# A transformer megakernel on one core: three rotating buffers for queries and keys, their low parts written in place, two for the rounded keys

## The reference, cut to what matters

```python
def _attn(q, k, v, mask):
    scale = 1.0 / np.sqrt(HD)
    s = jnp.einsum('bqhd,bkhd->bhqk', q, k) * scale
    s = jnp.where(mask, s, jnp.finfo(s.dtype).min)
    a = jax.nn.softmax(s, axis=-1)
    return jnp.einsum('bhqk,bkhd->bqhd', a, v)
```

## Time and profile before

| | |
|---|---|
| runs of the kernel | 1174.65, 1185.07, 1185.32 us (median 1185.07) |
| the profiled execution | 1176.95 us, its span 1174.8 us |
| PE busy | 1074.7 us (91% of the span), weight loads 725.9 us |
| DVE, ACT, POOL busy | 744.3, 622.1, 618.1 us |
| granted clock of PE | 0.856 of full on average |
| transfers on SP's queue | 24.3% of 16 engines' span |

### The profile page before, as it was taken

One profiled execution on the slowest core, in us unless ns is written; L12 is line 12 of the kernel. 1 busy time (PEld: TensorE's weight loads), 2 busy tenths in 40 slices (PEclk: granted clock), 3 DMA queues, 4 the chain that ended last, 5 costly groups with the idle time before them and its releaser, 6 DMA issues.

```text
span 1174.8 us, 32004 instructions
## 1 busy us (share of the span) xinstructions
PE 1074.7 (91%) x12961; PEld 725.9 (62%) x12961; DVE 744.3 (63%) x1852; ACT 622.1 (53%) x938; POOL 618.1 (53%) x739
## 2 busy tenths in 40 slices
PE   7898899989998999999999999889888988897998
PEld 5455555656666676676666566656555655565676
DVE  7757856767666443777778566767777754565521
ACT  2134434565656655454455455655556765654653
POOL 6657757665565432112226567665577553465531
PEclk9669968988777999999999667887889987876899
DMA  6423322332232102000000323232332323222101
GB/s 233 146 70 111 126 83 83 125 124 90 84 118 82 46 28 90 10 7 6 11 12 30 103 70 111 84 98 95 118 123 96 118 89 114 83 80 72 59 28 45
DMA packets 101459, 96.89 MB, mean 82 GB/s; under 512 B 11632, under 2 KB 93808, under 8 KB 100928
## 3 DMA queue, kind: packets, MB, share of 16 engines
q1 hardware_dynamic: 101312, 94.84, 24.3%
HBM read 18.77 MB, written 2.15 MB: 18 GB/s over the span
## 4 chain that ended last, share of the span: by engine, by line
PE 60%; POOL 12%; SPq 9%; issue 8%; DVE 6%; DMA 2%; ACT 2%; POOLq 0%; ACTq 0%; DVEq 0%
PE weighed L725 11%; PE scores L896 6%; PE row_scores L658 5%; PE weighed L748 5%; SPq L2135 4%; SPq L2138 4%; PE scores L695 4%; PE scores L613 3%; PE scores L710 3%; DVE negmax L1217 3%; PE row_scores L896 3%; PE quads L620 2%; POOL kblk_r L1927 2%; DMA q_ring<-qr 2%; PE quads L605 2%
## 5 line engine op out<-in xcount | busy, mean ns | idle before, releaser
L1217 DVE TENSOR_REDUCE negmax<-row_scores 128x8 f32<-128x616 f32 (+1 forms) x312 | 299.9, 961 | 248.7 <-PE row_scores L658 203.2
L1733 ACT ACTIVATE p<-scores 128x1024 f32<-128x1024 f32 (+1 forms) x253 | 251.6, 1019 | 145.3 <-PE scores L710 141.0
L1927 POOL TENSOR_TENSOR kblk_r<-work,pack_const 128x308 fp32r<-128x308 f32 (+1 forms) x160 | 133.9, 838 | 197.3 <-PE row_scores L658 183.2
L725 PE MATMUL weighed<-p,v 77*32 77x128 f32 (+1 forms) x5120 | 213.9, 319 | 2.1 <-DVE nat L1233 1.3
L725 PEld LDWEIGHTS weighed<-p,v 77*32 77x32 f32 (+1 forms) x5120 | 157.4, 127 | 57.9 <-issue 45.1
L658 PE MATMUL row_scores<-kblk_r,qr 32*128 32x308 f32 (+1 forms) x624 | 161.0, 511 | 16.6 <-DVE negmax L1217 13.4
L695 PE MATMUL scores<-q_ring,k_ring 32*77 32x128 f32 (+1 forms) x2512 | 136.4, 284 | 39.4 <-ACT p L1733 31.2
L695 PEld LDWEIGHTS scores<-q_ring,k_ring 32*77 32x77 f32 (+1 forms) x2512 | 112.1, 194 | 48.0 <-ACT p L1733 35.9
L658 PEld LDWEIGHTS row_scores<-kblk_r,qr 32*128 32x128 f32 x624 | 68.5, 214 | 104.1 <-DVE negmax L1217 49.9
L710 PE MATMUL scores<-nblk,select 32*77 32x512 bf16 (+1 forms) x628 | 104.2, 463 | 0.0
L1970 POOL TENSOR_TENSOR attn<-nat,rden 128x128 f32<-128x128 f32 x160 | 65.0, 406 | 61.5 <-DVE rden L1238 61.1
(11 more groups left out here) (334 smaller groups left out, 2027.4 us busy)
## 6 DMA issues: line engine op xcount, KB each, us to landing
q_ring<-work SPq DMA_DIRECT2D x160, 128.0 KB, 2.1
q_ring<-qr SPq DMA_DIRECT2D x160, 128.0 KB, 2.1
k_ring<-k_high SPq DMA_DIRECT2D x64, 128.0 KB, 2.1
k_ring<-work SPq DMA_DIRECT2D x64, 128.0 KB, 2.1
k_ring<-k_high SPq DMA_DIRECT2D x96, 77.0 KB, 2.0
k_ring<-work SPq DMA_DIRECT2D x96, 77.0 KB, 2.0
shared<-gates_hbm SPq DMA_DIRECT2D x24, 256.0 KB, 3.2
shared<-in_ctx_tok SPq DMA_DIRECT2D x15, 154.0 KB
```

The source lines that it names most:

```text
L725: mm = e.matmul(av_bank[TILE * j:TILE * j + TILE, i2 * S:(i2 + 1) * S], v[0:nk, at:at + TILE], p[n % 2][0:nk, g * NJ + j, :], start=i1 == ...
L1217: e.tensor_reduce(negmax[q % 2][:, 2 * h:2 * h + 2, s * NJ:(s + 1) * NJ], row_banks(n, h)[:, :, 0:NJ * nk].rearrange("p g (j k) -> p g j k ...
L1733: e.activation(p[n % 2][0:nk, 8 * h:8 * h + 8, :], score_banks(n, h)[0:nk].rearrange("p g (j q) -> p (g j) q", j=NJ), ACT.Exp, bias=hide, ...
L1927: e.tensor_tensor(kblk_r[n % 2][:, 0:NJ * nk].rearrange("p (j k) -> p j k", j=NJ), k_of[q % 2][:, s * nk:(s + 1) * nk].unsqueeze(1).to_bro ...
```

## The change

Queries and keys get three buffers each, used in turn (`q_of[q % 3]`, `k_of[q % 3]`), in the nine slices of `work` that held two each and the two low parts. The low part is written over the value itself. The rounded keys get two buffers of their own. What waited for the landing of the quad before (`round_k`, `split_q`, `split_k`) now waits for the quad two before (`round_k`), or for nothing of that kind (the splits); the writers of a buffer wait for the landing of the quad three before, through the new helper `stacked`. `split_k` now overwrites what `spread_k` reads, so it waits for the fourth `spread_k` of its quad. For the first quad of each phase it moves one slot later for that.

```diff
-        xn, q_of, k_of = [work[:, j, :] for j in range(3)], [work[:, 3 + j, :] for j in range(2)], [work[:, 6 + j, :] for j in range(2)]
-        q_low, k_low = work[:, 5, :], work[:, 8, :]
-        k_high = sb("k_high", [128, QUAD * S], F32R)
+        xn, q_of, k_of = ([work[:, 3 * i + j, :] for j in range(3)] for i in range(3))
+        k_high = [sb(f"k_high{i}", [128, QUAD * S], F32R) for i in range(2)]
...
+        def stacked(w, q):
+
+            for m in (2 * q, 2 * q + 1):
+                if m >= 0:
+                    w.wait_ge(*pair_landed(m))
...
             def rotate(q, which):
...
-                w.wait_ge(*freed)
-                if which:
-                    w.wait_ge(kblk_r_done, 4 * (q - 2) + 4)
+                stacked(w, q - 3)
...
             def round_k(q):
...
-                w.wait_ge(k_split, q)
-                if q:
-                    w.wait_ge(*pair_landed(2 * q - 2))
-                    w.wait_ge(*pair_landed(2 * q - 1))
-                e.copy(k_high[:, 0:cols], k_of[q % 2][:, 0:cols]).then_inc(k_rounded, 1)
+                w.wait_ge(k_split, q - 1)
+                stacked(w, q - 2)
+                e.copy(k_high[q % 2][:, 0:cols], k_of[q % 3][:, 0:cols]).then_inc(k_rounded, 1)
...
             def split_q(q):
                 w.wait_ge(qr_done, q + 1)
-                if q:
-                    w.wait_ge(*pair_landed(2 * q - 2))
-                    w.wait_ge(*pair_landed(2 * q - 1))
-                e.tensor_tensor(q_low, q_of[q % 2], qr[q % 3][:, :].bitcast(F32), ALU.subtract).then_inc(q_split, 1)
+                e.tensor_tensor(q_of[q % 3], q_of[q % 3], qr[q % 3][:, :].bitcast(F32), ALU.subtract).then_inc(q_split, 1)
 
             def split_k(q):
                 cols = QUAD * layer_of(q).nk
                 w.wait_ge(k_rounded, q + 1)
-                if q:
-                    w.wait_ge(*pair_landed(2 * q - 2))
-                    w.wait_ge(*pair_landed(2 * q - 1))
-                e.tensor_tensor(k_low[:, 0:cols], k_of[q % 2][:, 0:cols], k_high[:, 0:cols].bitcast(F32),
+                w.wait_ge(kblk_r_done, 4 * q + 4)
+                e.tensor_tensor(k_of[q % 3][:, 0:cols], k_of[q % 3][:, 0:cols], k_high[q % 2][:, 0:cols].bitcast(F32),
                                 ALU.subtract).then_inc(k_split, 1)
...
                     if t == 4 * lo - 5:
                         split_q(lo)
-                        split_k(lo)
-                    if cl == 0 and qi + 1 in quads and qi + 1 != lo:
-                        split_q(qi + 1)
+                    if cl == 0 and qi + 1 in quads:
+                        if qi + 1 != lo:
+                            split_q(qi + 1)
                         split_k(qi + 1)
```

More of the change, by code:

```diff
@@ L1184, in rotate @@
                 live = 0 if which == 0 else 1
-                dst = (q_of, k_of)[which][q % 2]
-                proj, freed = ((proj_q, (q_split, q - 1)), (proj_k, (k_split, q - 1)))[which]
+                dst, proj = ((q_of, proj_q), (k_of, proj_k))[which]
+                dst = dst[q % 3]
                 bank = k_bank(q) if which else quad_bank[:, :]
@@ L1208, in take_q @@
                 w.wait_ge(proj_q, q + 1)
-                w.wait_ge(q_split, q - 1)
-                e.tensor_scalar(q_of[q % 2], quad_bank[:, :], W[layer.name + "_qb"], None, ALU.add).then_inc(q_done, 1)
+                stacked(w, q - 3)
+                e.tensor_scalar(q_of[q % 3], quad_bank[:, :], W[layer.name + "_qb"], None, ALU.add).then_inc(q_done, 1)
             def row_max(n, h):
@@ L1645, in round_q @@
                 w.wait_ge(rows_done, 8 * (q - 3) + 8)
-                if q >= 3:
-                    w.wait_ge(*pair_landed(2 * (q - 3) + 1))
-                e.copy(qr[q % 3][:, :], q_of[q % 2]).then_inc(qr_done, 1)
+                stacked(w, q - 3)
+                e.copy(qr[q % 3][:, :], q_of[q % 3]).then_inc(qr_done, 1)
             def round_k(q):
@@ L1677, in take_k @@
                 w.wait_ge(proj_k, q + 1)
-                w.wait_ge(k_split, q - 1)
-                w.wait_ge(kblk_r_done, 4 * (q - 2) + 4)
+                stacked(w, q - 3)
                 if layer.mask == "kv":
-                    done = e.copy(k_of[q % 2][:, 0:cols], quad_bank[:, 0:cols])
+                    done = e.copy(k_of[q % 3][:, 0:cols], quad_bank[:, 0:cols])
                 else:
-                    done = e.activation(k_of[q % 2][:, 0:cols], quad_bank[:, 0:cols], ACT.Identity,
+                    done = e.activation(k_of[q % 3][:, 0:cols], quad_bank[:, 0:cols], ACT.Identity,
                                         bias=W[layer.name + "_kb"])
@@ L1688, in take_q @@
                 w.wait_ge(proj_q, q + 1)
-                w.wait_ge(q_split, q - 1)
+                stacked(w, q - 3)
                 if layer_of(q).gated:
-                    done = e.copy(q_of[q % 2], quad_bank[:, :])
+                    done = e.copy(q_of[q % 3], quad_bank[:, :])
                 else:
-                    done = e.activation(q_of[q % 2], quad_bank[:, :], ACT.Identity, bias=W[layer_of(q).name + "_qb"])
+                    done = e.activation(q_of[q % 3], quad_bank[:, :], ACT.Identity, bias=W[layer_of(q).name + "_qb"])
                 done.then_inc(q_done, 1)
@@ L1927, in spread_k @@
                 e.tensor_tensor(kblk_r[n % 2][:, 0:NJ * nk].rearrange("p (j k) -> p j k", j=NJ),
-                                k_of[q % 2][:, s * nk:(s + 1) * nk].unsqueeze(1).to_broadcast([128, NJ, nk]),
+                                k_of[q % 3][:, s * nk:(s + 1) * nk].unsqueeze(1).to_broadcast([128, NJ, nk]),
                                 W["own_head"].unsqueeze(2).to_broadcast([128, NJ, nk]), ALU.mult).then_inc(kblk_r_done, 1)
             def add_rotated(q, which):
-                dst = (q_of, k_of)[which][q % 2]
+                dst = (q_of, k_of)[which][q % 3]
                 w.wait_ge(rope_half, 4 * q + 2 * which + 2)
@@ L2133, in stack_pair @@
                 for x, (of_q, of_k) in enumerate(PARTS):
-                    k_src = k_low if of_k else k_high[:, :].bitcast(F32)
+                    k_src = k_of[q % 3] if of_k else k_high[q % 2][:, :].bitcast(F32)
                     e.dma_start(keys_of(m, nk)[x:128:NJ, :, :], k_src[:, k_at]).then_inc(landed, 16)
                 for x, (of_q, of_k) in reversed(list(enumerate(PARTS))):
-                    q_src = q_low if of_q else qr[q % 3][:, :].bitcast(F32)
+                    q_src = q_of[q % 3] if of_q else qr[q % 3][:, :].bitcast(F32)
                     e.dma_start(q_ring[m % PAIRS][x:128:NJ, :, :], q_src[:, q_at]).then_inc(landed, 16)
```

## The result

The changed kernel takes 1080.76 us (median of four executions, 1075.11 to 1112.75) against 1185.19 before; the ratio is 0.912, with a 95% interval of 0.905 to 0.920. The forecast was 1117, range 1092 to 1152: the direction was right, the size too small, and the range too high.

A forecast was written before the change was run, and what follows sets the result against it. It took an 18.6 us loop per quad, closed by `round_k`'s landing wait, to bound the kernel. From 1176.95 us, -31.2 - 1.9 - 59.5 + 25 + 7 + 1.3 = -59.3 gave 1117.7, stated as 1117, range 1092 to 1152.

The forecast's parts named there:

- The diagnosis: All quads: key split, transfer issues, landing, `round_k`, exponential and exact scores form a loop of 18.6 us, whatever PE's speed.
- (a): `round_k` waits for the quad two before: PE's 31.2 us of idle time before exact scores go; other bound 17.
- (e): Shorter quads meet smaller waits, `row_max` above all: 0.5 us in each of 14 quads, 7 us lost; bounds 0 and 20.
- (c): Eleven low-clock stretches behind the waits, 162.13 us together, return to full clock: 59.5 us gained; bounds 0 and 59.5.
- (d): Nine quads brought to full clock then pay 2.8 us each for a late normalised input: 25 us lost; bounds 0 and 45.
- (b): Start of phase 1: `exact(64)` no longer waits for an ACT instruction behind `round_k(17)`: 1.9 us gained, or 0.
- the wait costs twice: At `round_k`'s landing wait: the idle time, and then the same matmuls at the lower clock.
- a rival: Slower: narrow layers stay at low clock though PE is busy, as quad 17 did at 0.50; about 1200 us, chance 0.04.
- (f): Start of phase 0: `split_k(0)` moves behind the fourth `spread_k`, ahead of `normalise_x`: 1.3 us lost; other bound 0.
- (g): New buffer waits in `take_q`, `take_k`, `rotate`, and writing in place: nothing lost; in-place bound 0.1 us for each of 80.
- The idle time goes, the clock does not come back: Late inputs still lower the clock in every quad: 1136 us, or 1150 with no clock gain; chance 0.20.
- the full gain with nothing given back: All idle-time and clock gains come and late inputs cost nothing new: 1084 to 1095 us, chance 0.02.

The follow-up runs named there:

- one-wait kernel: The changed kernel, with only quad 17's `round_k` (start of phase 1) waiting for the landing of the quad before again: 1089.17 us, ratio 0.920.
- second profile: The changed kernel run once more with nothing altered, for another profile: median 1078.09 us, ratio 0.918; the profile's span is 1076.3 us.

## Why the prediction was wrong, step by step

**The diagnosis was right.** The loop of 18.6 us closed by `round_k` stood up: one line brings the old time back, relaxing that wait alone brings about 70% of the gain, and without it quad 34 of l3c takes 13.6 us.

**(a), (e), the idle time: right.** The sum had -31.2 - 1.9 + 7 + 1.3 = -24.8 us of idle time; measured -23.3. The cover for pair 2q held: no exact scores wait for a transfer. Of the waits that grew, the normalised input's did by 9.4 us and `row_max`'s by 2.1 (13.4 to 15.5), 11.5 together for the 7 us of (e), and mostly of another kind.

**(c) and (d), the clock: (d) is the step that failed.** I had -59.5 + 25 = -34.5 us; PE's busy time fell by 75.2. (c) was priced well. In l3s and l3c PE's busy time fell by 14.3 and 21.4 us, and the stretches priced in (c) were 11.0 and 20.6 there. Of the whole 75.2, 12.4 belong to quads 16 and 17 (43.05 to 30.68, see (b)); the other 62.8 are (c)'s 59.5 with nothing given back. The term that failed is (d), "given back". I had let nine quads with a late input pay 2.8 us each, 25 in all. Quads 9, 11, 23 and 37 of the changed kernel:

```profile
247.78:266.87 19.09, 18.05 (x269) 12.86 (x270) 12.04 (x32) 11.44 (x16) 11.31 (x16) 0.73 0.41 132
281.34:296.89 15.55, 14.31 (x274) 9.99 (x273) 14.34 (x42) 12.61 (x19) 13.43 (x19) 1.00 0.46 147
752.61:768.79 16.18, 14.50 (x252) 9.69 (x252) 15.05 (x32) 11.29 (x17) 12.61 (x15) 1.00 0.41 139
967.26:984.92 17.66, 15.52 (x249) 11.58 (x249) 12.01 (x32) 10.31 (x16) 12.56 (x17) 0.81 0.36 115
```

Quads 11 and 23 kept full clock, although PE waited 0.81 and 0.98 us for the input. So did quads 35 and 36, two of the nine, where no such wait came at all. Quads 9, 17 and 37 did run partly at the low clock (0.73, 0.68, 0.81), but they had run at 0.55, 0.50 and 0.61 before and are all shorter than they were; and in quad 37 what PE waited for was `row_max`, 0.89 us, not the input:

```profile
973.35 0.41 PE L663 MATMUL row_scores<-kblk_r,qr 32*128 32x308 f32 x2 [0.89 <-DVE negmax L1220]
```

The price as such was not too high: with the idle time filled (the kernel with four extra matmuls) quad 17 takes 15.33 us at 1.00 for 20.23, and quad 9 14.53 for 19.09. And quads 18 to 21, from which I had read it, pay in both kernels: 71.2 us for 73.2. What was wrong is to charge it as new to every quad that comes to full clock and normalises an input.

**(b), the start of phase 1: mis-sized, the second failure.** I priced it at the idle time, 1.9 us. The routed stage's end did come 1.8 us earlier, but quads 16 and 17 then took 34.4 us instead of 43.3 (12.4 us less of PE's busy time, with 3.5 more of idle time). The one-wait kernel shows that these 8.9 us hang on that wait. It was the rule that I had written at the top of the text (the wait costs twice), not applied to the second kind of place. I had even read quad 17 at 0.50 all through the earlier trace rows, and put it down to a rival. The forecast was 39 us over the second profile's time: 25 are (d), 12.4 the busy time of these two quads, and under 2 all the rest.

**(f), the start of phase 0: right in kind, a little small.** 1.8 us later for 1.3 in these two profiles; over all profiles 51.6 to 52.1 against 49.8 to 50.8.

**(g): right.** No wait for the landing of the quad three before shows in the list.

**The rivals.** "The idle time goes, the clock does not come back" was the opposite of what happened, and I gave it 0.20; the case that came, the full gain with nothing given back (1084 to 1095), had 0.02, and even its edge was above the 1081 measured. (d), (e) and (f) all stood on the side of a loss, and (d) was unproved; I had no term for a gain that I had overlooked.

The Trainium skill's rule ("TensorE: Matmul & The Clock Gate", section "HAM oscillation — how this bites in real kernels"; half of the throttled time, 81 us for the same stretches) would have given about 1096, nearer to the result, yet for the wrong reason. In l3c it would price the stretches at 25.8 us, and PE's busy time there fell by 21.4, near the 20.6 that follow from the 40% read from the slots.

What stays open is why the clock stays low for 30 to 60 us at the start of l0 in some executions and not in others of the same kernel; why it stays at 0.50 for 43 us in quads 16 and 17 with PE busy all but 0.2 us, once one wait stands before; and why a late input lowers it in some quads only.

## What to carry to other kernels

When a queue of short transfers feeds a buffer that is rewritten each round, look for the one wait on a busy in-order engine that closes the loop, add up the loop's own length, and compare it with the length of a round in which the wait is absent: the difference is about the gain a round, with clock and all (here 5.0 us a quad in quad 34, and 4.6 on average over seven quads of l3c). Then look for the other waits on the same landing: here the splits' cost 30 us once `round_k`'s was gone. Idle time often brought a low clock behind it here, so price every wait with both, at a phase's start too, and let a give-back into the sum only if the quads in question do not pay it already. After such a change, the work that the single buffer had forced into one slot can move: here the earlier split of the queries gave a further 3%.

## What the runs showed of the hardware

The size of the clock's share: of the 98.5 us between the two spans, 75.2 are the same 12961 matmuls running at a higher granted clock. Groups of four extra matmuls in idle gaps (0.9 us a group) took l2 from 0.86 to 1.00 and shortened it by 16.2 us. PE being busy did not bring it back: quads 16 and 17 ran at 0.50 for 43.3 us with 0.2 us idle. An idle time of 0.8 us before five of the transposes did not lower the clock in l3s, where 10.5 of 128.2 us are idle at 1.00, while l2 with 13.2 of 136.9 us idle ran at 0.86. The length of one wait does not decide it alone: before the transposes of quads 9 and 11 PE waited 0.86 and 0.81 us, and quad 9 ran at 0.73 on average, quad 11 at 1.00.
